# Self-attention in a decoder layer: the product with the values by high and low parts, own block everywhere plus a triangle with the blocks' difference

## The reference, cut to what matters

```python
scores = jnp.einsum('bhtd,bsd->bhts', q, k) * scale        # 16 heads of 128, one key and value head
scores = jnp.where(mask[None, None], scores, -1e30)        # 0 <= t - s < 128
probs = jax.nn.softmax(jnp.concatenate([scores, sink], axis=-1), axis=-1)
attn = jnp.einsum('bhts,bsd->bhtd', probs[..., :t], v)
```

## Time and profile before

| what | value |
|---|---|
| median of 3 runs | 1639.65 us (1635.01 to 1639.69) |
| the profiled execution | 1639.33 us, of it a span of 1637.5 us |
| busy: PE, DVE, ACT, POOL | 1555.2, 1224.0, 1185.7, 1271.3 us of the span |
| self-attention steps (first to last `inv_den`) | 83.1 to 586.9 us |
| granted TensorE clock over the span | 0.99 of full speed |

### The profile page before, as it was taken

How to read it: one execution, slowest core, us unless ns; L and a number is a source line. 1 busy time by engine, 2 the same in 40 slices (tenths; PEclk the granted TensorE clock), 3 DMA queues, 4 the chain that set the end, 5 groups by cost and what they waited for, 6 DMA issues and landing times. The chain is left out here.

```text
span 1637.5 us, 23915 instructions
## 1 busy us (share of the span) xinstructions
PE 1555.2 (95%) x7487; PEld 1070.2 (65%) x7520; DVE 1224.0 (75%) x2240; ACT 1185.7 (72%) x1962; POOL 1271.3 (78%) x1142
## 2 busy tenths in 40 slices
PE   8899999999999988999999999999999969999996
PEld 3478777877787755666566666666656526666664
DVE  2489989878877756787877788778888556767765
ACT  2355556777755435999999889989998837878875
POOL 0387787787777714899989999999999938888880
PEclk9999999999999998999999999999999999999999
DMA  7224241433330105211312032102202130100100
GB/s 247 105 65 101 70 92 56 109 123 115 117 114 15 33 22 153 58 45 26 107 39 63 20 106 61 33 20 48 69 13 87 75 115 1 40 27 26 33 14 26
DMA packets 57190, 110.24 MB, mean 67 GB/s; under 512 B 9244, under 2 KB 13596, under 8 KB 56682
## 3 DMA queue, kind: packets, MB, share of 16 engines
q1 hardware_dynamic: 55488, 107.64, 22.2%
q10 hardware_dynamic: 1578, 1.07, 0.2%
HBM read 71.26 MB, written 18.88 MB: 55 GB/s over the span
## 5 line engine op out<-in xcount | busy, mean ns | idle before, releaser
L1421 POOL TENSOR_TENSOR x_p_lo<-x_p,x_p_hi 128x1024 fp32r<-128x1024 f32 x256 | 606.3, 2396 | 62.5 <-ACT x_p_hi L1201 39.4
L1334 DVE TENSOR_REDUCE x_maxes<-x_ps_a 128x1 f32<-128x1024 f32 x252 | 306.6, 1217 | 121.2 <-PE x_ps_a L1521 117.0
L1164 ACT ACTIVATE x_p<-x_ps_b,x_any_valid 128x1024 f32<-128x1024 f32 x256 | 285.0, 1113 | 58.5 <-PE x_ps_b L1501 53.8
L1201 ACT ACTIVATE x_p_hi<-x_p 128x1024 fp32r<-128x1024 f32 x256 | 271.2, 1059 | 6.3
L1501 PE MATMUL x_ps_b<-x_Q,x_K 103*128 103x512 f32 x512 | 218.9, 509 | 7.2 <-ACT x_p L1164 5.6
L1555 PE MATMUL x_ps_o<-x_p_hi,x_V 128*96 128x512 f32 x512 | 208.9, 408 | 2.5 <-POOL x_p_lo L1421 2.5
L1556 PE MATMUL x_ps_o<-x_p_lo,x_V 128*96 128x512 f32 x512 | 201.6, 394 | 0.0
L1521 PE MATMUL x_ps_a<-x_K,x_Q 99*128 99x512 f32 x504 | 166.8, 412 | 11.4 <-DVE x_maxes L1334 8.4
L443 ACT ACTIVATE a_aT_hi<-a_ps_a 128x512 fp32r<-128x512 f32 x64 | 38.3, 598 | 175.1 <-PE a_ps_a L726 142.0
L1501 PEld LDWEIGHTS x_ps_b<-x_Q,x_K 103*128 103x128 f32 x512 | 88.2, 191 | 98.1 <-issue 56.0
L1521 PEld LDWEIGHTS x_ps_a<-x_K,x_Q 99*128 99x128 f32 x504 | 88.5, 190 | 54.5 <-DVE x_maxes L1334 32.1
(11 more groups left out here) (286 smaller groups left out, 4000.9 us busy)
## 6 DMA issues: line engine op xcount, KB each, us to landing
shared<-in_L_ffn_w_gate SPq DMA_DIRECT2D x16, 512.0 KB, 4.2
shared<-in_L_ffn_w_up SPq DMA_DIRECT2D x16, 512.0 KB, 4.1
shared<-in_L_ffn_w_down SPq DMA_DIRECT2D x16, 512.0 KB, 4.4
shared<-in_ctx SPq DMA_DIRECT2D x8, 1024.0 KB, 7.6
x_scratch<-rows SPq DMA_DIRECT2D x31, 256.0 KB, 2.0
x_Q<-x_q_hi SPq DMA_DIRECT2D x112, 64.0 KB, 2.0
shared<-in_L_attn_out_w SPq DMA_DIRECT2D x6, 1024.0 KB, 8.4
ffn_quant<-shared SPq DMA_DIRECT2D x24, 256.0 KB, 4.4
```

The lines of the kernel that those rows point to most:

```text
L1164: act.activation(p[:, v % 3, :, :], ps_b[:, :, :], ACT.Exp, scale=any_valid[:, b % 2:b % 2 + 1]).then_inc(exp_ready, 1)
L1201: act.activation(p_hi[:, r], p[:, v % 3], ACT.Copy).then_inc(hi_ready, 1)
L1334: dve.tensor_reduce(out=maxes[:, c % 2, 3 + r:4 + r], in_=scores_bank(n)[:, :, :], axis=mybir.AxisListType.XY, op=ALU.max).then_inc(max_re ...
L1421: pool.tensor_tensor(out=p_lo[:, v % 3], in0=p[:, v % 3], in1=p_hi[:, r].bitcast(F32), op=ALU.subtract).then_inc(lo_ready, 1)
```

## The change

The product with the values is written as two parts. The first multiplies all 128 places with the own block's values. The second corrects the places that belong to the block before: the triangle `prev_part` of the probabilities times dv, the values of the block before minus the own ones. Both parts are split into high and low parts and take three float32r matmuls each, in place of one float32 matmul each.

For that v, dv and their parts are made once per tile: v_hi and dv_hi on ScalarE, dv, v_lo and dv_lo on GpSimd. Per step, `pT_own` goes; `pT_hi` (ScalarE, after `sink_exp`) and `pT_lo` (VectorE, at the end of its round, behind `inv_den`) split the transposed probabilities; `pT_prev_hi` (VectorE, from PSUM, in the old place) and `pT_prev_lo` (VectorE, from `pT_lo` in SBUF, last of its round) take the triangle of both, in two-block steps alone. The sum of absolute weights of rounds 0 to 23 moves from VectorE to ScalarE, where it stands behind `pT_hi` and ahead of the copy of q. `v`, `dv` and `q_t` now lie in the free part of `work`.

```diff
+        v = work[:, 1024:1408].rearrange("p (s n) -> p s n", s=3)
+        dv = work[:, 1408:1536]
+        q_t = work[:, 1536:2048].rearrange("p (j a n) -> p j a n", j=G1, a=2)
...
-        v = sb("v", [P, TPB, P])
+        v_hi = sb("v_hi", [P, 2, P], F32R)
...
-        pT_own = sb("pT_own", [P, G1 * P])
-        pT_prev = sb("pT_prev", [P, G1 * P])
+        pT_hi = sb("pT_hi", [P, G1 * P], F32R)
...
+        def two_block_tiles(t):
+
+            return t - (t + TPB - 1) // TPB
...
@@ -411,9 +425,10 @@
                     if t:
                         act.wait_ge(qckT_made, t)
                     act.activation(qck[:, :], ps_front[:, 0:2 * P], ACT.Copy).then_inc(qck_ready, 1)
-                    if t >= 4:
-                        act.wait_ge(a_made, 4 * (t - 2))
-                    act.activation(v[:, t % TPB, :], ps_front[:, 2 * P:3 * P], ACT.Copy).then_inc(v_ready, 1)
+                    if t >= 3:
+                        act.wait_ge(v_lo_ready, t - 2)
+                        act.wait_ge(dv_ready, two_block_tiles(t - 1))
+                    act.activation(v[:, t % 3, :], ps_front[:, 2 * P:3 * P], ACT.Copy).then_inc(v_ready, 1)
                     act.wait_ge(qck_ready, t + 1)
                     act.activation(k_sq[:, :], qck[:, P:], ACT.Square, accum_out=k_ss[:, 0:1]).then_inc(k_ss_ready, 1)
                 t = tile_of(c, 4)
@@ -455,6 +470,28 @@
                                        bias=neg_max[:, c % 2, j:j + 1], accum_out=row_sum[:, c % 2, j:j + 1]).then_inc(exp_ready, 1)
                     act.wait_ge(sink_arg_ready, c + 1)
                     act.activation(sink_exp[:, c % 2, :], sink_arg[:, c % 2, :], ACT.Exp).then_inc(sink_exp_ready, 1)
+                if 0 <= c - 1 < STEPS:
+                    k = c - 1
+                    act.wait_ge(pT_made, k + 1)
+                    if k:
+                        act.wait_ge(a_made, k)
+                    if len(blocks(k // 4)) == 2:
+
+                        act.wait_ge(pT_prev_hi_ready, two_blocks(k + 1))
+                    act.activation(pT_hi[:, :], ps_pT[:, :], ACT.Copy).then_inc(pT_hi_ready, 1)
+                t = tile_of(c, 1)
+                if t is not None:
+                    act.wait_ge(v_ready, t + 1)
+                    if t >= 2:
+                        act.wait_ge(a_made, 4 * (t - 1))
+                    act.activation(v_hi[:, t % 2, :], v[:, t % 3, :], ACT.Copy).then_inc(v_hi_ready, 1)
+                t = tile_of(c, 0)
+                if t is not None and t % TPB:
+                    act.wait_ge(dv_ready, two_block_tiles(t + 1))
+                    act.activation(dv_hi[:, t % 2, :], dv[:, :], ACT.Copy).then_inc(dv_hi_ready, 1)
+                if 0 <= c < FFN_CHUNKS:
+                    act.wait_ge(f_abs_in[c % 4], 16 * (c // 4 + 1))
+                    act.activation(f_abs[:, c % 4, :], f_abs[:, c % 4, :], ACT.Abs, accum_out=f_part[:, c:c + 1]).then_inc(f_part_ready, 1)
                 if 0 <= c - 24 < FFN_CHUNKS:
                     k = c - 24
                     act.wait_ge(f_round_ready, k + 1)
@@ -560,26 +597,18 @@
                     dve.wait_ge(qT_hi_ready, k + 1)
                     dve.tensor_tensor(out=qT_lo[:, k % 2], in0=ps_qT[:, :].rearrange("p (a b) -> p a b", a=G1),
                                       in1=qT_hi[:, k % 2].bitcast(F32), op=ALU.subtract).then_inc(qT_lo_ready, 1)
-                if 0 <= c - 1 < STEPS:
+                if 0 <= c - 1 < STEPS and len(blocks((c - 1) // 4)) == 2:
                     k = c - 1
                     dve.wait_ge(pT_made, k + 1)
-                    if k:
-                        dve.wait_ge(a_made, k)
-                    dve.tensor_tensor(out=pT_own[:, :].rearrange("p (a b) -> p a b", a=G1), in0=ps_pT[:, :].rearrange("p (a b) -> p a b", a=G1),
-                                      in1=own_part, op=ALU.mult).then_inc(pT_own_ready, 1)
-                    if len(blocks(k // 4)) == 2:
-                        dve.tensor_tensor(out=pT_prev[:, :].rearrange("p (a b) -> p a b", a=G1), in0=ps_pT[:, :].rearrange("p (a b) -> p a b", a=G1),
-                                          in1=prev_part, op=ALU.mult).then_inc(pT_prev_ready, 1)
+                    dve.wait_ge(a_made, k)
+                    dve.tensor_tensor(out=pT_prev_hi[:, :].rearrange("p (a b) -> p a b", a=G1), in0=ps_pT[:, :].rearrange("p (a b) -> p a b", a=G1),
+                                      in1=prev_part, op=ALU.mult).then_inc(pT_prev_hi_ready, 1)
                 if 0 <= c + 2 < STEPS:
                     k = c + 2
                     dve.wait_ge(q_sq_ready, k + 1)
                     dve.tensor_reduce(out=q_ss[:, k % 2, :], in_=q_sq[:, :, :], axis=AXX, op=ALU.add).then_inc(q_ss_ready, 1)
                     dve.wait_ge(q_ss_ready, k + 1)
                     dve.tensor_scalar(q_ss[:, k % 2, :], q_ss[:, k % 2, :], P * EPS_RMS, None, ALU.add).then_inc(q_eps_ready, 1)
-                    if 0 <= c < FFN_CHUNKS:
-                        dve.wait_ge(f_abs_in[c % 4], 16 * (c // 4 + 1))
-                        dve.tensor_reduce(out=f_part[:, c:c + 1], in_=f_abs[:, c % 4, :], axis=AXX, op=ALU.add,
-                                          apply_absolute_value=True).then_inc(f_part_ready, 1)
                     if c in (8, 16, 24):
                         m = c // 8 - 1
                         dve.wait_ge(f_part_ready, 8 * m + 8)
@@ -596,6 +625,17 @@
                 if 0 <= c < STEPS:
                     dve.wait_ge(den_ready, c + 1)
                     dve.reciprocal(inv_den[:, c % 2, :], den[:, c % 2, :]).then_inc(inv_ready, 1)
+                if 0 <= c - 1 < STEPS:
+                    k = c - 1
+                    dve.wait_ge(pT_hi_ready, k + 1)
+                    if k:
+                        dve.wait_ge(a_made, k)
+                    dve.tensor_tensor(out=pT_lo[:, :], in0=ps_pT[:, :], in1=pT_hi[:, :].bitcast(F32), op=ALU.subtract).then_inc(pT_lo_ready, 1)
+                    if len(blocks(k // 4)) == 2:
+                        dve.wait_ge(pT_lo_ready, k + 1)
+                        dve.tensor_tensor(out=pT_prev_lo[:, :].rearrange("p (a b) -> p a b", a=G1),
+                                          in0=pT_lo[:, :].bitcast(F32).rearrange("p (a b) -> p a b", a=G1),
+                                          in1=prev_part, op=ALU.mult).then_inc(pT_prev_lo_ready, 1)
 
         @block.gpsimd
         def _(pool):
@@ -649,6 +689,21 @@
                     k = c + 2
                     pool.wait_ge(q_eps_ready, k + 1)
                     pool.tensor_tensor(out=q_r[:, k % 4, :], in0=q_ss[:, k % 2, :], in1=half_neg[:, :], op=ALU.pow).then_inc(q_r_ready, 1)
+                t = tile_of(c, 1)
+                if t is not None:
+                    if t % TPB:
+                        pool.wait_ge(v_ready, t + 1)
+                        if two_block_tiles(t):
+                            pool.wait_ge(dv_lo_ready, two_block_tiles(t))
+                        pool.tensor_tensor(out=dv[:, :], in0=v[:, (t - 1) % 3, :], in1=v[:, t % 3, :], op=ALU.subtract).then_inc(dv_ready, 1)
+                    pool.wait_ge(v_hi_ready, t + 1)
+                    pool.tensor_tensor(out=v_lo[:, t % 2, :], in0=v[:, t % 3, :], in1=v_hi[:, t % 2, :].bitcast(F32), op=ALU.subtract)\
+                        .then_inc(v_lo_ready, 1)
+                t = tile_of(c, 0)
+                if t is not None and t % TPB:
+                    pool.wait_ge(dv_hi_ready, two_block_tiles(t + 1))
+                    pool.tensor_tensor(out=dv_lo[:, t % 2, :], in0=dv[:, :], in1=dv_hi[:, t % 2, :].bitcast(F32), op=ALU.subtract)\
+                        .then_inc(dv_lo_ready, 1)
 
         @block.tensor
         def _(pe):
@@ -717,13 +772,18 @@
                 if 0 <= c - 2 < STEPS:
                     k = c - 2
                     blk = blocks(k // 4)
-                    pe.wait_ge(pT_own_ready, k + 1)
+                    t = k // 4
+                    pe.wait_ge(pT_lo_ready, k + 1)
                     if k:
                         pe.wait_ge(aT_lo_ready, k)
-                    last = pe.matmul(ps_a[:, :], v[:, blk[-1], :], pT_own[:, :], start=True, stop=len(blk) == 1)
+                    if k % 4 == 0:
+                        pe.wait_ge(v_lo_ready, t + 1)
+                    last = three(ps_a[:, :], v_hi[:, t % 2, :], v_lo[:, t % 2, :], pT_hi[:, :], pT_lo[:, :], True, len(blk) == 1)
                     if len(blk) == 2:
-                        pe.wait_ge(pT_prev_ready, two_blocks(k + 1))
-                        last = pe.matmul(ps_a[:, :], v[:, blk[0], :], pT_prev[:, :], start=False, stop=True)
+                        if k % 4 == 0:
+                            pe.wait_ge(dv_lo_ready, two_block_tiles(t + 1))
+                        pe.wait_ge(pT_prev_lo_ready, two_blocks(k + 1))
+                        last = three(ps_a[:, :], dv_hi[:, t % 2, :], dv_lo[:, t % 2, :], pT_prev_hi[:, :], pT_prev_lo[:, :], False, True)
                     last.then_inc(a_made, 1)
                 if 0 <= c + 1 < STEPS:
```

(25 more changed lines are left out.)

## The result

The changed kernel takes 1647.94 us (median of 5 runs, 1644.48 to 1649.8), the kernel before 1639.69 us on the same chip (5 runs, 1635.01 to 1640.22). The ratio is 1.0053 (1.0034 to 1.0072), so the change costs 8.3 us or 0.5%. The prediction said 1653.5, inside 1631 to 1667. The direction and the place of the loss hold. The size does not: 8.3 us against the 14.4 of its sum.

What follows compares the result with a forecast made beforehand. TensorE was taken to set the stage's pace, with the chain from placed to aT_lo nearly as long. Savings and delays summed to +14.4 us on 1639.33, giving 1653.7, stated as 1653.5 us, range 1631 to 1667.

Steps and rivals of the forecast that it cites:

- TensorE: Value products: three float32r matmuls per float32 one take 17.3 us off TensorE's queue, of which 12.7 us can be collected.
- The walk through phase 3: Rounds of remainder 3 mod 4: late statistics put sink_arg at 7.3 us, pT_lo's end at 8.9, pT_prev_lo's at 10.0.
- The link: End of VectorE's round: pT_lo waits for pT_hi behind sink_exp, which waits for GpSimd's sink_arg; that lateness reaches TensorE.
- Phase 0: Rounds divisible by 4: placed starts at 2.7 us, not 1.62; +0.8 us a round, +1.25 in rounds 25 to 48.
- Phase 1: Rounds of remainder 1 mod 4: late kT_hi delays placed; +0.9 us with clipping pass, +1.6 with absolute sum.
- The drain: Stage's end, after the last pT transposes: three operations in a row instead of two, against a shorter product; +0.9 us.
- Free port: Rival, 17%: pT_prev_lo on VectorE doesn't wait for GpSimd; some +8 us, 1645 us (1639 to 1649).
- Slower still: Rival, 13%: behind pT_prev_lo, q_r gets the port ahead of f_quant in rounds 25 to 48; +8.4 us, 1662 us.
- Covered: Rival, 20%: VectorE catches up, so the chain through sink_arg doesn't get late; about -6.5 us, 1633 us.
- The sum as forecast: Whole stage: +7 us in rounds 0 to 24, +7 in 25 to 48, -0.5 in 49 to 63, +0.9 at the end; +14.4.

Runs made afterwards that it cites:

- experiment 1: Kernel before, each float32 product with the values replaced by three float32r products from the same high parts, no low parts made: 1628.62 us, ratio 0.9938.
- experiment 10: Changed kernel with only pT_hi moved ahead of sink_exp on ScalarE, VectorE's order kept: 1651.71 us, ratio 1.0079.
- experiment 6: Changed kernel with pT_hi ahead of sink_exp on ScalarE, and pT_lo and pT_prev_lo ahead of inv_den on VectorE: 1655.51 us, ratio 1.0105.
- experiment 7: Changed kernel with pT_hi, qcT_hi and kT_hi ahead of sink_exp, and pT_lo and pT_prev_lo ahead of inv_den: 1643.3 us, ratio 1.0031.
- experiment 8: Kernel of experiment 3 with, only in rounds of remainder 3, pT_hi ahead of sink_exp and pT_lo, pT_prev_lo ahead of inv_den: 1636.83 us, ratio 0.9990.
- experiment 2: Changed kernel with pT_prev_lo reading PSUM in place of pT_lo in SBUF, so the triangle's low part is left out: 1637.43 us, ratio 0.9997.
- experiment 5: Changed kernel without the operation pT_prev_lo; TensorE's three products take pT_prev_hi instead: 1636.16 us, ratio 0.9986.
- experiment 3: Changed kernel with qcT_hi and kT_hi on ScalarE moved one round earlier, right behind dv_hi: 1637.76 us, ratio 0.9994.
- experiment 4: Changed kernel with pT_prev_lo reading PSUM (low part left out) and qcT_hi and kT_hi one round earlier: 1630.51 us, ratio 0.9949.
- experiment 9: Changed kernel with the sum of absolute weights of rounds 0 to 23 back on VectorE: 1650.55 us, ratio 1.0073.

## Why the prediction was right or wrong, point by point

**TensorE: right.** Six float32r matmuls follow each other 0.235 apart, and the transposes of q start 2.84 into an undisturbed round. Alone it gives 12.2 us in the stage and 10.3 in the median (experiment 1) against 12.7.

**The walk through phase 3: right to 0.2 us.** In round 43 `sink_arg` came at 7.18 (forecast 7.3), `sink_exp` ended at 7.62 (7.7), `pT_hi` at 8.11 (8.2), `pT_lo` at 8.83 (8.9), the scaling at 9.23 (9.35), `pT_prev_lo` at 9.78 (10.0).

**The link: half of it.** The prediction led the delay through `sink_exp`, `pT_hi`, `pT_lo`. A second way, through `sink_exp`, `den`, `inv_den`, `pT_lo`, is just as long and holds `pT_lo` without the first (experiment 10). Both end at 439.63 in round 43, so the walk came out right with one of them overlooked, and that is luck. Whether the first alone would hold `pT_lo` as long was not tried. The half link misled every reordering: in experiments 6, 7 and 8 whatever held `inv_den` back went into GpSimd's queue and came back a round later.

**Phase 0: the term that was mis-sized.** Forecast +0.8 a round, and +1.25 in rounds with `f_quant`. Rounds 28, 40 and 44, which have it, measured +0.76, +0.49 and +0.77; rounds 8, 12 and 24, without it, +0.05, +0.28 and +0.60. In round 44 the walk would have put `placed` at 2.7 + 0.45 = 3.15, and it came at 2.68. Of these 0.47 us, 0.25 are `pT_prev_lo`'s end, 2.30 into the round and not 2.55 (it took 0.91, not the 1.1 that a full wait for the scaling made). `f_quant` added 0.33 (441.35 to `placed` at 441.68), not 0.45; the other 0.1 is a gap that the walk allowed behind `pT_prev_lo`. In rounds 8 and 12 `placed` came at 1.96 and 2.20, not at 2.7, since `sink_exp` ended at 7.23 in round 7 and 7.48 in round 11, before the 7.62 of round 43. Sum of phase 0: +3.5 measured, +7.2 forecast; this is the largest part of the surplus.

**Phase 1: right for most rounds.** `placed` of round 45 came at 3.07 and its output product at 5.98, forecast 6.0. Rounds 29, 41 and 45 measured +0.92, +0.94 and +0.94 and round 37 +1.08 (forecast +0.9), rounds 9 and 13 +1.26 and +1.29 (forecast +1.6). Of the three rounds beside single-block tiles, forecast at +1.0, round 21 measured +1.04, but rounds 5 and 17 only +0.06 and +0.18.

**The drain: wrong sign.** Forecast +0.9, measured -0.74; experiment 1, without the new operations, has -0.81. The three operations in a row are hidden there, and the shorter product shows.

**The start: not foreseen.** Rounds 1 and 2 are longer by 1.5 and 2.9 us, and the prediction has no term for them. The busy time by stretch gives the granted clock in its eighth entry. The kernel before:

```profile
84.00:90.00 6.00, 5.31 (x31) 4.70 (x30) 5.63 (x14) 3.75 (x14) 4.98 (x9) 0.74 0.23 79
90.00:96.00 6.00, 6.00 (x33) 5.03 (x33) 5.76 (x14) 3.32 (x13) 5.50 (x8) 1.00 0.27 89
```

The changed kernel:

```profile
84.00:90.00 6.00, 4.70 (x18) 3.89 (x18) 4.32 (x13) 4.48 (x15) 5.16 (x9) 0.50 0.19 66
90.00:96.00 6.00, 6.00 (x26) 5.42 (x27) 4.42 (x11) 3.55 (x13) 3.96 (x8) 0.63 0.25 87
96.00:102.00 6.00, 6.00 (x36) 5.37 (x35) 2.42 (x7) 2.54 (x8) 5.55 (x9) 1.00 0.25 87
```

TensorE's clock is at its lower level (1.2 GHz) for all of 84 to 90 us, and back at 2.4 GHz only in the course of 90 to 96. Before, it was back by 90. Ahead of its return stands a longer wait for `kT_hi`. In round 1 of the kernel before VectorE showed this:

```profile
84.30 0.29 DVE L524 TENSOR_TENSOR a_qcT_lo<-a_ps_front,a_qcT_hi 128x128 fp32r<-128x128 f32 x1 [1.06 <-ACT a_kT_hi L430]
```

and after the change:

```profile
83.86 0.29 DVE L561 TENSOR_TENSOR a_qcT_lo<-a_ps_front,a_qcT_hi 128x128 fp32r<-128x128 f32 x1 [2.10 <-ACT a_kT_hi L445]
```

From 81 to 88 us TensorE was busy 6.59 us before and 4.81 after. The traces of all twelve kernels sort the same way. Where `kT_hi` and the absolute sum both stand as in the changed kernel (that kernel and experiments 2, 5, 6 and 10), the lower level lasts to between 94 and 97 us, and rounds 1 and 2 cost 4.4 to 4.9 us. In the other seven (the kernel before, experiments 1, 3, 4, 7, 8 and 9) it ends between 84 and 89 us, and these rounds cost at most 1.0. So a late `kT_hi` at the start goes together with a late clock. No run held the one fixed and changed the other. The stage starts 1.9 us earlier than before, but so it does by 0.5 to 2.1 us in all eleven kernels of this study, which says more of the one profiled execution of the kernel before than of the change.

**The rivals.** *Free port* was given 1645, measured with the port free it is 1637.4. It was to keep +0.43 in each phase 0, and rounds 28 to 44 lie up to 0.2 below the kernel before; and it priced nothing for the shorter `q_r`. So the port was taken to be worth 8.5 us and is worth 9 to 10.5. *Slower still* fell: `f_quant` took 0.41 to 0.43 in all 24 rounds, so `q_r` never got ahead of it. Nor did `f_quant` hold `q_r` up: `q_r` took 1.46 to 1.48 behind `pT_prev_lo` in the rounds without `f_quant` as well. *Covered* fell with the wait for `aT_lo`.

**The sum as forecast.** Its items for rounds 25 to 48 add up to +6.0, not to the +7 that was written; with the +6.9 of rounds 0 to 24 the walk gives some +13.3, not +14.4. The stage measured +9.5. For rounds 0 to 24 the forecast of +7 stands beside a measured +7.3, which is luck: 4.4 us of that are rounds 1 and 2, which it did not have, and the other rounds cost 2.9. Rounds 25 to 48 measured +4.5, the last rounds -1.6 in place of -0.5, and the drain -0.7 in place of +0.9.

**The sum as measured**, in the stage. TensorE alone gives -12.2 (experiment 1). Rounds 1 and 2 cost +4.4. In the other rounds the port and `kT_hi` together cost 14.3 (experiment 4; one by one 9.2 and 7.0, since part of what they cost is shared). The remaining 2.9 are the operations themselves; experiment 5, 2.7 us below experiment 2 in these rounds, puts most of it on the 0.7 us of `pT_prev_lo`, if its difference is carried over. -12.2 + 4.4 + 14.3 + 2.9 = +9.4, the 9.5 measured but for rounding. These are single executions. By medians against the kernel before on the same chip it is -10.3 for TensorE, +16.9 for the port and `kT_hi` with the start, and +1.6 for the rest, +8.3 in all.

## What to carry to other kernels

Before an operation is hung behind another engine's result, look for what stands ahead of it in its own queue: here `inv_den` was a gate just as late as the new operand, and moving the new work in front of it made the other engine late instead. An operation of VectorE with both inputs in SBUF beside a busy GpSimd is to be priced on both engines, and with all that is queued behind the GpSimd operation. When work is appended to a queue's end, the first small operation of the next round that someone waits for (`kT_hi` here, 0.28 us long and worth 10 us, a third of it in two rounds at the start) is the one to move or to protect.
